# Two grouped convolutions and two expert-mixed 1x1 layers on one core: how the experts' rows and the second layer's taps are loaded

## The reference, cut to what matters

```
def conv_layer(x, c, weight, c_weight, bias):            # layers 0 and 2
    out = conv1d(x, weight, padding=4, groups=4)         # weight 128 x 32 x 9
    return out + (c @ c_weight.T)[:, :, None] + bias[None, :, None]

def expert_layer(x, emb, W0, b0, W1, b1, W2, b2, weight, bias_k):   # layers 1 and 3
    h = gelu(emb @ W0 + b0); h = gelu(h @ W1 + b1)
    att = softmax(h @ W2 + b2)                           # 128 batches x 8 experts
    agg_w = einsum('bk,koi->boi', att, weight[..., 0])   # a 128 x 128 matrix for each batch
    return einsum('boi,bih->boh', agg_w, x) + (att @ bias_k)[:, :, None]

x = x + conv_layer(x, ...)      # then expert_layer, conv_layer, expert_layer, each added to x
```

## Time and profile before

| | us |
|---|---|
| median of the three runs | 2518.91 |
| the profiled execution's own time | 2525.17 |
| its span in the trace | 2523.4 |
| PE busy in the span | 2478.9 (98%) |
| DVE busy | 2138.9 (85%) |
| ACT busy | 1518.8 (60%) |
| POOL busy | 48.1 (2%) |

### The profile page before, as it was taken

How to read it: one execution, slowest core, us unless ns; L and a number is a source line. 1 busy time by engine, 2 the same in 40 slices (tenths; PEclk the granted TensorE clock), 3 DMA queues, 4 the chain that set the end, 5 groups by cost and what they waited for, 6 DMA issues and landing times.

```text
span 2523.4 us, 99058 instructions
## 1 busy us (share of the span) xinstructions
PE 2478.9 (98%) x45240; PEld 1486.6 (59%) x45240; DVE 2138.9 (85%) x799; ACT 1518.8 (60%) x1113; POOL 48.1 (2%) x27
## 2 busy tenths in 40 slices
PE   7799999999999999999999999999999999999998
PEld 3344444455555555556666666666666666666664
DVE  4788988888888888888888888898898898898883
ACT  4356666666666666666666666666666666666664
POOL 1500000000000000000000000000000000000000
PEclk7899999999999999999999999999999999999999
DMA  8554444444544544544544534534534444434433
GB/s 235 185 168 126 159 131 126 160 129 127 161 128 127 161 127 129 160 126 131 159 125 133 158 125 135 156 125 136 155 125 139 152 125 141 150 125 143 148 94 118
DMA packets 186066, 357.23 MB, mean 142 GB/s; under 512 B 12770, under 2 KB 143850, under 8 KB 153194
## 3 DMA queue, kind: packets, MB, share of 16 engines
q1 hardware_dynamic: 185512, 354.53, 45.2%
q10 hardware_dynamic: 522, 2.20, 0.5%
HBM read 205.69 MB, written 150.99 MB: 141 GB/s over the span
## 4 chain that ended last, share of the span: by engine, by line
PE 96%; DMA 2%; POOL 1%; ACT 0%; POOLq 0%; issue 0%; SPq 0%; ACTq 0%; DVE 0%
PE psum L346 60%; PE psum L412 35%; POOL prod_w L271 1%; DMA y<-experts 1%; DMA prod_w<-conv_w 1%; PE psum L322 0%; DMA mix_dram<-shared 0%; POOL mixw L268 0%; POOLq L45 0%; PE psum L306 0%; ACT shared L543 0%; SPq L198 0%; DVE y L708 0%; ACT outb L595 0%; ACT y L574 0%
## 5 line engine op out<-in xcount | busy, mean ns | idle before, releaser
L346 PE MATMUL psum<-diff,prod_w 32*64 32x512 f32 x28672 | 1695.5, 589 | 17.3 <-POOL prod_w L273 11.1
L346 PEld LDWEIGHTS psum<-diff,prod_w 32*64 32x64 f32 x28672 | 961.0, 131 | 644.2 <-issue 307.2
L649 DVE TENSOR_TENSOR diff<-xin 128x2052 f32<-128x2052 f32 x256 | 995.2, 3942 | 302.8 <-PE psum L346 299.9
L412 PE MATMUL psum<-y,mixw 32*64 32x512 f32 x16384 | 1030.5, 590 | 5.5 <-DVE y L708 4.3
L412 PEld LDWEIGHTS psum<-y,mixw 32*64 32x64 f32 x16384 | 577.7, 132 | 347.3 <-issue 191.4
L649 DVE TENSOR_TENSOR diff<-x 128x2055 f32<-128x2055 f32 x256 | 572.3, 2315 | 6.4 <-ACT x L613 6.4
L613 ACT ACTIVATE x<-psum,bias_now 128x2048 f32<-128x2048 f32 x128 | 252.7, 1974 | 203.1 <-PE psum L412 203.1
L595 ACT ACTIVATE outb<-psum,bias_now 128x2048 f32<-128x2048 f32 x128 | 252.2, 1970 | 200.1 <-PE psum L412 191.5
L563 ACT COPY shared<-psum 128x2048 f32<-128x2048 f32 x128 | 239.0, 1867 | 194.8 <-PE psum L346 194.8
L706 DVE TENSOR_TENSOR y<-y,shared 128x2048 f32<-128x2048 f32 x128 | 295.2, 2306 | 37.7 <-ACT y L572 37.7
L708 DVE TENSOR_TENSOR y<-y,shared 128x2048 f32<-128x2048 f32 x128 | 295.3, 2307 | 1.0 <-ACT y L574 1.0
(11 more groups left out here) (56 smaller groups left out, 94.5 us busy)
## 6 DMA issues: line engine op xcount, KB each, us to landing
xin<-x SPq DMA_DIRECT2D x128, 1024.0 KB, 6.9
out<-outb SPq DMA_DIRECT2D x128, 1024.0 KB, 4.8
mixw<-mix_dram SPq DMA_DIRECT2D x512, 128.0 KB, 5.2
mix_dram<-shared SPq DMA_DIRECT2D x8, 1024.0 KB, 5.8
mix_dram<-y SPq DMA_DIRECT2D x8, 1024.0 KB, 6.0
y<-experts ACTq DMA_DIRECT2D x2, 512.0 KB, 10.7
prod_w<-conv_w SPq DMA_DIRECT2D x4, 256.0 KB, 14.1
diff<-expert_rows ACTq DMA_DIRECT2D x4, 144.0 KB
```

What stands on the lines that cost most here:

```text
L346: return pe.matmul(psum[cols, half, g, :], prod_w[v][at, kind, s, cols], moving, start=start, stop=stop, skip_group_check=True)
L412: mm = pe.matmul(psum[cols, half, r, :], mixw[m][at, b, g, cols], y[m][at, :, g, b, :], start=g == 0, stop=g == GROUPS - 1)
L649: nc.vector.tensor_tensor(into(kind), in0, in1, op).then_inc(diff_ready[v], 1)
```

## The change

`rows[m]` was loaded by four DMAs, one for each quarter r: nine partitions that lie side by side, 16 KB for each. It is now loaded by nine DMAs, one for each expert and one for the identity: four partitions, one in each quarter, 16 KB for each. The host lays out the array as (9, 4, 4096) instead of (9, 16384), with the same bytes.

`rows[0]` was loaded on ACT's queue, between the two `experts` loads. It is now the first thing on SP's queue, ahead of SP's wait for `wide`. `load_taps(1)` stood after the load of x for the second pair. It now stands after the fourth store of layer 1's matrices. `load_rows(1)` stood after the eighth store and now stands after the seventh. PE's waits count the nine DMAs.

```
-                for r in range(PH):
-                    sp.dma_start(rows[m][CG * r:CG * r + EXPERTS + 1, :],
-                                 expert_rows[m][:, r * SLICE:(r + 1) * SLICE]).then_inc(rows_loaded[m], 16)
+                for k in range(EXPERTS + 1):
+                    sp.dma_start(rows[m][k::CG, :], expert_rows[m][k]).then_inc(rows_loaded[m], 16)
...
+            load_rows(0)
             sp.wait_ge(par_loaded, 16)
             load_taps(0)
             load_x(0)
             for j in range(SETS):
                 sp.wait_ge(first_taken, j + 1)
                 sp.dma_start(columns_of(0, j), first_home[j]).then_inc(first_stored[j], 16)
-            load_rows(1)
+                if j == 3:
+                    load_taps(1)
+                if j == 6:
+                    load_rows(1)
             sp.wait_ge(taps_ready, 1)
             for j in range(SETS):
                 sp.wait_ge(first_stored[j], 16)
             load_mix(0, 0)
             sp.wait_ge(diff_ready[0], PRODUCTS)
             load_x(1)
-            load_taps(1)
...
-            pe.wait_ge(rows_loaded[0], 16 * PH)
+            pe.wait_ge(rows_loaded[0], 16 * (EXPERTS + 1))
...
-                    pe.wait_ge(rows_loaded[1], 16 * PH)
+                    pe.wait_ge(rows_loaded[1], 16 * (EXPERTS + 1))
...
-            for r in range(PH):
-                act.dma_start(rows[0][CG * r:CG * r + EXPERTS + 1, :],
-                              expert_rows[0][:, r * SLICE:(r + 1) * SLICE]).then_inc(rows_loaded[0], 16)
...
-        return np.concatenate([w, eye[None]], axis=0).reshape(w.shape[0] + 1, -1)
+        return np.concatenate([w, eye[None]], axis=0).reshape(w.shape[0] + 1, 4, -1)
```

## The result

The changed kernel ran in 2526.02 us (median of 20), the kernel before in 2520.6 (median of 20): ratio 1.0020, interval 1.0014 to 1.0027, +5.4 us, a small loss that the interval sets apart from none. Of the 10.0 us between 2516.0 and 2526.02, 1.7 are the base, which is 2520.6 over the 20 runs.

What follows compares the result with a forecast made beforehand. It took PE as the bound in steady state, so only idle time in the first 140 us could be gained: PE passes L563 3.9 us earlier, less 1.0 for the clock, net -2.9 from 2518.9 to 2516.0; range 2510 to 2525.

Steps and rivals of the forecast that it cites:

- the gain of the taps: Ahead of conv(1, 0): taps loaded earlier remove PE's 11.1 us wait for POOL, at 2.1 us of transfer ahead of later stores.
- the clock: Conv(1, 0) to steady state: PE's stops cost clock speed; taken as 1.0 us lost, bounds 0 and 3.4.
- the start: Up to the first convolution: rows[0] lands at 17.0 against 18.01, and everything there comes 0.8 us earlier.
- the point at which PE passes L563: After 15 of conv(1, 0)'s 28 sets, PE needs ACT's copy L563; forecast 114.7 against 118.65, so -3.9 us.
- That the taps are late and POOL is held by DVE: Second layer's taps land only at 72.42, and L271 on POOL takes 21.66 us while DVE works almost without pause.
- 8.0 up to the next wait: In conv(1, 0): without any other shift PE passes ACT's copy L563 8.0 us earlier, not 11.1.
- X + 40.2: When PE passes L563: 40.2 us after X, the landing of the second pair's x, since DVE is busy from then on.
- Nine rounds in 9.0 us for `rows[1]`: The new row load: nine DMAs on four engines, 1.0 us a round at a total rate of 66 GB/s.
- The eighth store at 63.6: Landing of the eighth store: 53.3 - 0.8 (start) + 2.1 (taps) + 9.0 (rows[1] ahead of it).
- X 10.9 us after it: Second pair's x lands 10.9 us after the eighth store: 2.6 + 0.9 issues, 6.0 for x, 1.4 for matrices; X = 74.5.
- the row loads become the bound: Rival, chance 0.12: 1.5 us a round, both row loads take 13.5 us; +5.4 us, 2524.3, deciding from about 1.2 a round.
- `wide` is held back: Rival, chance 0.13: rows ahead of `wide` make it land at 12.2, the second L306 at 24.6; 2521.3 us.

Runs made afterwards that it cites:

- e2: The kernel before with only the second layer's taps moved behind the fourth store; 2521.31 us against 2521.34, ratio 0.9998.
- e1: The kernel before with only rows[0] loaded by nine DMAs of four partitions at the front of SP's queue; 2524.31 us against 2521.34, ratio 1.0012.
- b1: The kernel before with only the second layer's taps moved behind the second store of layer 1's matrices; 2520.33 us against 2522.09, ratio 0.9993.
- before_again_2: The kernel before, unchanged, profiled a third time; 2521.68 us in that one execution, with no wait for POOL.
- after_again_1: The changed kernel, unedited, profiled a second time; 2526.81 us in that one execution.
- e6: The kernel before with rows[0] at the front of SP's queue, by the old four DMAs of nine partitions; 2521.44 us against 2522.05, ratio 1.0000.
- a2: The changed kernel with every transfer in its new place, but both row loads by the old four DMAs; 2521.34 us against 2520.31 before, ratio 1.0005.
- b2: The kernel before with rows[0] at SP's front by the old four DMAs and the taps behind the second store; 2520.57 us against 2520.31, ratio 1.0000.
- e8: The kernel before with rows[1] loaded by 18 DMAs of two partitions 32 apart, in the old place; 2526.32 us, executed once.
- e4: The changed kernel with rows[0] back on ACT's queue by four DMAs of nine partitions; 2522.22 us against 2521.34 before, ratio 1.0002.
- e5: The kernel before with rows[0] loaded by nine DMAs of four partitions, still on ACT's queue; 2527.12 us against 2522.05, ratio 1.0020.

## Why the prediction was wrong, point by point

Two terms of the sum failed. By the experiments the larger is the gain of the taps: -5.9 us in the sum with its price, -4.9 with the clock, 0.0 in e2 (interval -2.8 to +2.0). The other is the start: -0.8 in the sum, +3.0 in e1 and +3.6 in the profile of the changed kernel. Against the forecast of -2.9 the measured +5.4 is 8.3 off. By the profiles 5.5 of it is the point at which PE passes L563, worked out below, and 0.3 the clock; 2.4 is how much further the first profile of before lies above its median than that of the changed kernel.

- **That the taps are late and POOL is held by DVE**: right, and the move ends it. **That 11.1 us, or 8.0 up to the next wait, are there to be gained**: failed. It took one profiled execution as the kernel. The four profiles have 11.1, 6.3, none and 11.1. Where this wait is short, others come up, and e2 measured 0.0. Its sentence that the 2525.17 differs from the median by "the setup", which "carries over unchanged", was the place to see it: of its 4.6 us over the median of 20, 2.0 lie in the first 140 us, against the mean of the four profiles.
- **The next wait is ACT's L563, and PE passes it at X + 40.2**: right in kind. X was 80.77 and PE went on at 120.21, X + 39.4; the wait itself was only 0.25, as PE had stood before for 3.80 us on DVE's work on the same x (98.27). In b1 and `before_again_2` it is 2.6 and 3.2.
- **The start, 0.8 us earlier**: wrong by 4.4, the largest part of the 5.5. I had `rows[0]` land at 17.0; PE got it at 21.55. And I let the first experts load wait for nothing; PE waited 3.6 us for it. The sum had begin 2.3, rounds 9.0, other loads on the four engines 4.2, landing 1.5. By the packets it was 3.5, 10.2 (nine of 1.13 us on each engine), 6.7 in which these engines did other work or stood, and 1.2. So a row itself took hardly longer than in `rows[1]` (1.13 and 1.08); what was too small is mostly the share of the other loads, `wide`, both experts loads, the taps and x, on the engines that all rows had to go through.
- **Nine rounds in 9.0 us for `rows[1]`**: 9.9, near. **The eighth store at 63.6**: 67.5, which is the start (+4.4), the rounds (+0.9) and 1.4 less than the sum for the rest. **X 10.9 us after it**: 13.3, +2.4. I took 6.0 us for x, and its two loads took 7.2 and 10.8; two stores of 1 MB are issued right behind them, at 70.34, and their packets run beside x's from 77.1. That these are the cause was not tested. In `after_again_1` it was 12.3. X was 80.77, beyond the 78 that the prediction had named as a sign of being wrong. Together PE passes the point 5.5 us later than forecast: 4.4 + 0.9 - 1.4 + 2.4 - 0.8.
- **The clock, +1.0**: from the point to the first long piece PE needed 20.9 us, before 19.5: +1.3, with a granted clock of 0.84 where it was 0.91.
- **The rivals**: "the row loads become the bound" is what happened, at 1.1 us a round, below the 1.2 that I had put as its threshold, because the start alone crossed it. Its total of +5.4 is the measured one by luck: it had `rows[1]` take 13.5 us (9.9), and between the first profiles of the two kernels the change costs 3.0. "`wide` is held back" happened in e6, a2 and b2 (6.8 to 8.7 us) with the old layout, and cost nothing. By the rule of the ports in the Trainium skill (SBUF — State Buffer, "Door 1: The DMA port swizzle") a round was to take 1.2 us, an estimate from the page's rate for a port, and the sum to be no change. The round is near the 1.1 that the packets have, but e8 contradicts the sharing that it was worked out from: two rows on partitions 32 apart took 0.61 to 0.64 us.

What stays open: what lengthens x's way after the store, what holds row loads at 54 to 66 GB/s, why e1's loss does not show in the first 140 us of its profile, and why three kernels whose profiles show steady state 2 us earlier than the mean of the four profiles of before (e4, a2, b2) measure 0.3 to 1.0 us slower. One profile each is too few for the last two.

## What to carry to other kernels

Compare the profiled execution's own time with the median before pricing a wait in it: where it stands several us above, profile again. Price the wait over several profiles, and by when the work behind it starts, not by its length: here a wait 8 us shorter let steady state start 3.6 us earlier. A wait that two engines' lock decides is a draw and not a property. And before rows are spread over more DMAs with fewer partitions each, count the engines that one DMA uses: here the bytes per engine, beside what else those engines carried, set when the last row landed, and not the spread over the partitions.

## What the runs showed of the hardware

- The same program waited 11.1, 6.3, 0 and 11.1 us for POOL's last combination in four executions (the last three on one chip). L271 before it took 21.7, 4.5, 1.5 and 21.6 us.
- The nine DMAs of four partitions all ran on four engines: four row packets in flight, DMA share 0.47 (changed kernel, 54.4 to 64.6).
- Partitions 32 apart were loaded as fast as partitions 64 apart (two rows of 16 KB in flight, 0.61 to 0.64 and 0.61 us while alone; 0.88 and 0.83 us a round over the whole load).
- A row of 16 KB took 0.61 us with two in flight, 1.1 with four, 2.2 with nine.
- Nine DMA issues cost ACT 4.89 us and four cost 1.46; its first activation came 3.5 us later (e5).
- A parameter load that landed 2.6 to 4.5 us late (e6, a2) cost nothing that could be measured: in e6 the rows and both experts loads were there when PE asked, and the time was -0.6 us against before.
